# In the attention of a graph network, GpSimd waits for the queries of the group two places back ahead of every second group's gathers

## The reference

```
def sage_conv(x, src, dst, W_l, b_l, W_r, n_nodes):
    msgs = x[src]
    agg = segment_sum(msgs, dst);  cnt = segment_sum(ones, dst)
    return (agg / max(cnt, 1)) @ W_l.T + b_l + x @ W_r.T

x = layernorm(x + sage_conv(relu(sage_conv(x, ...)), ...))

# attention: 4 heads of 16 features
Qh, Kh, Vh = x @ Wq.T + bq, x @ Wk.T + bk, x @ Wv.T + bv     # per node
Ee = edge_attr @ We.T + be                                    # per edge
score = exp(clip((Kh[src] * Qh[dst] / sqrt(16) * Ee).sum(-1), -5, 5))
wV = segment_sum(Vh[src] * score, dst)
x = layernorm(x + wV)
```

## Time and profile before

| | |
|---|---|
| median of 3 runs | 13896.76 us (13885.14 to 13908.0) |
| profiled execution | 13876.17 us, its span 13874.4 us |
| POOL busy | 7767.2 us (56%) |
| PE busy, weight loads busy | 7655.9 us (55%), 6718.6 us (48%) |
| DVE busy, ACT busy | 4877.0 us (35%), 2823.4 us (20%) |
| granted TensorE clock, mean of the span | 0.614 |

### The profile page before, as it was taken

One profiled execution on the slowest core, in us unless ns is written; L12 is line 12 of the kernel. 1 busy time (PEld: TensorE's weight loads), 2 busy tenths in 40 slices (PEclk: granted clock), 3 DMA queues, 4 the chain that ended last, 5 costly groups with the idle time before them and its releaser, 6 DMA issues.

```text
span 13874.4 us, 192542 instructions
## 1 busy us (share of the span) xinstructions
PE 7655.9 (55%) x51633; PEld 6718.6 (48%) x51634; DVE 4877.0 (35%) x11774; ACT 2823.4 (20%) x4770; POOL 7767.2 (56%) x8221
## 2 busy tenths in 40 slices
PE   5556656566666555566655555444444544444554
PEld 4555545555555445455544545444444444444444
DVE  3333333333333323233333334333333333433334
ACT  1111111111111000000000003333333333333333
POOL 5555655555555555555555555555555555555554
PEclk7666666766666666666666666555555555555555
DMA  3222222222222112111111112333333333333333
GB/s 62 50 55 52 53 50 50 49 50 49 49 49 49 42 41 46 41 42 43 41 40 41 40 40 82 101 97 98 101 95 98 98 99 90 101 92 93 99 93 82
DMA packets 951617, 917.13 MB, mean 66 GB/s; under 512 B 484896, under 2 KB 740544, under 8 KB 950544
## 3 DMA queue, kind: packets, MB, share of 16 engines
q0 software_dynamic: 260000, 369.16, 12.8%
q1 hardware_dynamic: 605345, 430.43, 11.6%
q10 hardware_dynamic: 85325, 105.63, 2.2%
HBM read 789.35 MB, written 115.24 MB: 65 GB/s over the span
## 4 chain that ended last, share of the span: by engine, by line
PE 30%; issue 30%; another core or an unknown queue 23%; DVE 7%; DVEq 7%; ACT 2%; ACTq 0%; DMA 0%; POOL 0%; POOLq 0%; SPq 0%
PE ps_kv L763 4%; PE ps_kv L754 3%; PE ps_e L740 3%; PE ps_sum L723 2%; PE ps_q L723 2%; PE ps_kv L923 2%; PE ps_hot L723 2%; PE ps_t L732 1%; ACT node_q L1037 1%; PE ps_kv L772 1%; PE ps_sum L923 1%; PE ps_hot L923 1%; PE ps_kv L903 1%; PE ps_q L923 1%
## 5 line engine op out<-in xcount | busy, mean ns | idle before, releaser
L627 POOL DMA_INDIRECT kv<-kv_rows,src_ids x3125 | 2955.6, 946 | 2344.0 <-DVE message L1520 1412.2
L627 POOL DMA_INDIRECT kv<-in_x,src_ids x2500 | 2365.3, 946 | 1845.4 <-issue 912.1
L627 POOL DMA_INDIRECT kv<-h_rows,src_ids x2500 | 2367.1, 947 | 1801.5 <-issue 955.6
L754 PE MATMUL ps_kv<-between,hot 128*128 128x490 bf16 x2500 | 897.8, 505 | 976.2 <-ACT node_q L1037 553.9
L723 PE MATMUL ps_sum<-kv,hot 128*128 128x65 f32 x5000 | 937.9, 355 | 247.7 <-issue 210.5
L723 PEld LDWEIGHTS ps_sum<-kv,hot 128*128 128x128 f32 x5000 | 922.8, 277 | 270.9 <-issue 270.2
L1086 ACT ACTIVATE node_h<-node_h,unit 128x640 bf16<-128x640 f32 x722 | 1042.6, 1444 | 36.9 <-issue 8.1
L723 PE MATMUL ps_hot<-kv 128*128 128x65 f32 x1880 | 418.9, 400 | 1075.4 <-issue 885.8
L723 PEld LDWEIGHTS ps_hot<-kv 128*128 128x128 f32 x1880 | 391.7, 309 | 1148.8 <-issue 1146.7
L754 PEld LDWEIGHTS ps_kv<-between,hot 128*128 128x128 bf16 x2500 | 291.4, 130 | 1305.9 <-issue 995.8
L1306 DVE TENSOR_SCALAR between<-ps_t,message 128x980 bf16<-128x980 f16 x1250 | 898.7, 719 | 0.0
(11 more groups left out here) (253 smaller groups left out, 12432.2 us busy)
## 6 DMA issues: line engine op xcount, KB each, us to landing
node_h<-in_dst SPq DMA_DIRECT2D x625, 320.0 KB
node_q<-in_edge_attr SPq DMA_DIRECT2D x125, 480.0 KB
edge_space<-ee_rows SPq DMA_DIRECT2D x125, 480.0 KB
kv<-kv_rows,src_ids POOLq DMA_INDIRECT x3125
kv<-in_x,src_ids POOLq DMA_INDIRECT x2500
node_q<-in_edge_attr SPq DMA_DIRECT2D x125, 320.0 KB
kv<-h_rows,src_ids POOLq DMA_INDIRECT x2500
edge_space<-ee_rows SPq DMA_DIRECT2D x125, 320.0 KB
```

Source lines behind the costliest of these rows:

```text
L627: nc.gpsimd.indirect_dma_start(out=into_slot, out_offset=None, in_=table_rows, in_offset=bass.IndirectOffsetOnAxis(ap=ids, axis=0),).then_ ...
L754: mm = nc.tensor.matmul(bank, place_hot[:, k, :], pair_hot[:, k, half * HALF * W:(half + 1) * HALF * W], start=(k == 0), stop=(k == K - 1))
```

## The change

Inside POOL's ring, for the attention alone (`phase == 2`), and only for the places 2, 4, ..., 24 of a ring of 25, a wait on `att.query` stands ahead of the wait on `att.message`. Place 0 has no such wait, and neither have the odd places. With T rings done, T * RING + (at - 1) queries are those of all groups up to the one two places back.

```
--- before.py
+++ after.py
@@ -648,6 +648,8 @@
                             at = j * slots + u
 
 
+                            if phase == 2 and at and at % 2 == 0:
+                                pool.wait_ge(p.query, T * RING + (at - 1))
                             if not (first_slots_free and at < SLOTS):
                                 pool.wait_ge(through, T * (SUBS * slots) + at + 1)
                                 hold(pool)
```

## The result

| | kernel before | changed kernel |
|---|---|---|
| median of 4 runs, us | 13,890.95 (13,830.82 to 13,908.0) | 13,470.49 (13,461.65 to 13,476.19) |
| ratio, 95% interval | | 0.9698 (0.9681 to 0.9716) |
| profiled span, us | 13,874.4 | 13,466.0 |

A forecast was written before the change was run, and what follows sets the result against it. Slow issue during long gather bursts was taken to bound the attention. Bursts of three groups plus pairs gave 8.38 us a group against 8.51, 81 us saved; 13795 and 13816 gave the middle, 13805 us, range 13610 to 14010.

The forecast's parts named there:

- The slow issue as what bounds the attention: Attention, 8.51 us a group: while gathers run on, all other engines issue slowly, from some 5 to 8 us into a burst.
- The wait costs nothing by itself, the gathers being early: Attention: gathers were issued 40.7 us ahead of their scores, so delaying them by some microseconds has no direct cost.
- the 15 us that I set as the floor: Attention: the lead of a group's gathers over its scores should stay above 15 us.
- A pair takes 15.65 us, with 3.45 us idle: Attention: two groups' gathers, then POOL idle until PE's second step ends 14.9 us after the start; 7.8 us a group.
- 15% of the pairs fail by a stop that is too short: Attention: 15% of 57 pairs stop too briefly for issue to recover, each costing 4.55 us more, 39 us in all.
- The rival of the short stop: POOL's stop ahead of even groups is too short; at half failing the attention takes 200 us more, 14075; chance 0.32.
- 30 of 87 starts go on past ten gathers: Attention: 16 bursts of three groups at 25.5 us each and 14 at 26.5, beside 57 pairs.
- the second L919: End of PE's second step after a burst's start, giving the queries awaited; within 9.7 us, the wait would be already met.
- The sum: Attention: 1710 us for 204 groups, 8.38 us a group, 0.13 us less than before, 81 us over 625 groups.
- "much faster" rival: Attention: bursts of 15 and lone groups vanish, nearly all go as pairs, 7.83 us a group; 13,660 us; chance 0.13.
- The marks to look for: Attention trace: some 200 waits on L919 or unnamed, message waits under 100, tens commonest, 50 or 12 weight loads after stops.
- The Trainium skill's rule: Instruction fetch is by DMA and "mostly hidden", so gathers would not starve PE and the wait would change nothing: 13876.

The follow-up runs named there:

- one place back: The changed kernel with even groups' gathers waiting for the queries of the group one place back instead of two: 13,417.52 us, ratio 0.9673 to the kernel before.
- the bare pauses: The kernel before plus a pause of six small iotas on GpSimd ahead of every second group's attention gathers, no added wait: 13,437.43 us, ratio 0.9682.

## Why the prediction was wrong

- *The slow issue as what bounds the attention.* Right, and now shown: a pause without any dependency gives the same gain, and a chip without the slow issue runs the attention in 3,901 us.
- *The wait costs nothing by itself, the gathers being early.* Right: mean lead 23.2 us after. The smallest fell to 9.2 us, under the 15 us that I set as the floor, but no wait of VectorE's scores for a gather is named in the changed kernel's view of waits. With one place back there are 62, 237.3 us, and with the bare pauses 308, 1317.2 us (rows below), and neither was slower. My reading, which no run tests, is that VectorE would have waited there for something else in the slow issue anyway.

```profile
DVE ps_t L1513 <- DMA kv<-kv_rows,src_ids: 237.3, 62, 7.6
```

```profile
DVE ps_t L1520 <- DMA kv<-kv_rows,src_ids: 1317.2, 308, 8.1
```

- *A pair takes 15.65 us, with 3.45 us idle.* Right in size: the 243 bursts of ten took 15.55 us in the mean, with a stop of 3.25 us in the median behind them. In part this is luck. I had the stop end with a query that comes late, and in 154 of 291 waits it ended with the register instruction, the query being there.
- *15% of the pairs fail by a stop that is too short.* Too many. A short stop does fail (behind that of 1.53 us above, the next pair started only 16.55 us later), but of the 294 idle times over 0.4 us among the attention's gathers only 11 were under 2.5 us. The rival of the short stop did not come about, because a query that is there early does not shorten the stop below some 3 us: the register instruction is held until 2.0 to 2.5 us after the last gather. And 2.85 us would have sufficed: behind each of 18 stops of 2.7 to 3.0 us came 40 matmuls or more in seven us.
- *30 of 87 starts go on past ten gathers.* This is the step that failed, and in it the sentence that where the second L919 comes early "the new wait would find its condition met and the burst goes on". I had 16 of 87, 18%, with the second L919 within 9.7 us, and let 34% run to three groups. In the changed kernel the second query came that early in 127 of 274 bursts of at least ten, 46% (43% of the 144 that began less than 1.2 us after an L921), far more often than I had it, and yet only 30 bursts of 282, 11%, were longer than ten. Of these 30, 20 are the fifteens at the ring's end, which I had overlooked, and 10 are bursts that went on through a wait. A wait that is met in the middle of a burst stops GpSimd all the same. I had carried over from the waits for messages that a met wait costs nothing; for the wait for queries that held, in the changed kernel, only in a burst's first 3 us, and on the chip without the slow issue throughout.
- *The sum.* With these two terms at nothing, no burst going on and no pair failing, the working of the "much faster" rival gave 7.83 us a group, and 7.86 was measured. This agreement is close by luck too: pairs were 0.1 us shorter than its 15.65, and the bursts at the ring's end, which it did not have, took 24.8 us for three groups. It had a chance of 0.13. Its time was put at 13,660, half of the way, though its own terms gave 425 us; the range cut it off at 13,610.
- *The marks to look for.* Waits with TensorE's line or without a name: 220 (200 said). Waits for messages: 72 (under 100 said). Tens commonest: yes. Weight loads in the seven us behind a stop, from the changed kernel: 47 after the stop of 4.35 us and 6 after that of 1.53 us (about 50 and 12 said):

```profile
8628.80:8635.80 7.00, 1.56 (x6) 1.53 (x6) 2.13 (x6) 2.71 (x4) 5.47 (x6) 0.50 0.39 83
8645.30:8652.30 7.00, 5.44 (x46) 5.10 (x47) 4.49 (x11) 5.44 (x8) 5.48 (x6) 0.50 0.32 93
```

- *The Trainium skill's rule* ("Runtime: NRT & Kernel Launch", section "Instruction fetch mechanics": to go on to the next block of instructions costs "one DMA tail-bump, mostly hidden"). From it I worked out a time of 13,876, and 13,470 was measured. What failed is my step from the page to the time, not the page: I took it that if fetch does not starve TensorE, the gathers do not either. The trace shows next to no fetch in the attention. This is the instruction queue's row from 8600 to 13700 us in the kernel before (packets, MB, share of 16 DMA engines), where the slow issue comes with every long burst; in the first summing pass, from 1000 to 3800 us, the two instruction queues have 317 packets:

```profile
q14 instruction: 2, 0.02, 0.0%
```

So the engines are not waiting for a refill of instructions by DMA there. My picture of a store that runs out after some 50 to 65 matmuls describes the counts and names no part of the chip; the cause stays open.

## What to carry to other kernels

Where the compute engines thin out together while GpSimd issues indirect gathers, count what they get through in a burst, not the time: if bursts of any length let through one fixed number, let the starting engine stop after just the work which that number covers, for as long as the recovery takes. A wait for an event is no such stop by itself. Look in the trace at what it does when it is already met: here the message wait let GpSimd go on, so bursts grew to twenty, and the query wait, on a register instruction, stopped it for 3 us even so. The query wait cost nothing on the chip without the effect, where a fixed pause costs its length. And do not carry the behaviour of one wait over to another, or count only starts of the trace of before: check in the code which places have no such wait, and put a bare pause beside the wait to see whether it is the event or the stop that helps.

## What the runs showed of the hardware

- The same kernel takes 13,734 to 13,897 us on five occasions and 10,445 us on another chip, at the same 944 to 946 ns for a gather and with a granted clock near 0.5 in the attention on both. What differs between the traces is the slow issue of TensorE, VectorE and ScalarE during bursts of indirect gathers. Which property of the chip or its surroundings decides it is open. All times on record come with a granted clock, so from executions that the profiler recorded; whether the slow issue is there without the recording was not tried.
- Where it exists, it holds GpSimd's register instruction with the query wait as well: in 154 of 291 cases until some 2 to 2.5 us after the last gather's end, though the query was done. It did not hold the message wait (339 of 345 went on).
- Where it exists, TensorE gets 53 to 57 matmuls in the median through a burst of 12.2 to 31 us. Behind ten gathers, a stop under 1.5 us was followed by 5 matmuls (median) in the next seven us, one of 2.3 to 2.5 us by 26, one of 3.3 to 3.6 us by 46.
- Neither the bytes of the gathers (an eighth: 0.9999) nor those of SyncE's broadcasts (1.0005) matter to it, and in the attention it comes with 2 packets of instruction fetch in 5,100 us.
- GpSimd issues a direct DMA of the same 128 rows in 535 ns, an indirect one in 944.
